# A decoder layer with 64 experts: the first gathers read the token names directly, and most first weights are loaded behind a wait for them

## The reference

```
x = x + self_attention(layernorm(x))
x = x + cross_attention(layernorm(x), ctx, mask)
x = x + ffn(layernorm(x))

ffn:  scores = softmax(x @ gate.T)                 # 64 experts, 8 groups, 3 groups and 6 experts kept
      buf[e, slot] = x[token]                      # at most 192 tokens of each expert
      out[e] = (silu(buf[e] @ Wg[e].T) * (buf[e] @ Wu[e].T)) @ Wd[e].T      # 512 -> 352 -> 512
      y = sum over the 6 experts of out[expert, slot] * weight
      shared = silu(x @ Sg.T) * (x @ Su.T) @ Sd.T  # 512 -> 704 -> 512, for every token
```

## Time and profile before

| what | value |
|---|---|
| median of the runs | 1560.71 us |
| profiled execution | 1567.02 us |
| its span | 1565.3 us |
| mean granted TensorE clock | 0.98 |
| TensorE busy | 1480.1 us (95%) |
| VectorE, ScalarE, GpSimd busy | 72%, 61%, 46% |
| DMA | 280.25 MB, mean 179 GB/s |

### The profile page before, as it was taken

How to read it: one execution, slowest core, us unless ns; L and a number is a source line. 1 busy time by engine, 2 the same in 40 slices (tenths; PEclk the granted TensorE clock), 3 DMA queues, 4 the chain that set the end, 5 groups by cost and what they waited for, 6 DMA issues and landing times.

```text
span 1565.3 us, 30313 instructions
## 1 busy us (share of the span) xinstructions
PE 1480.1 (95%) x10344; PEld 1223.1 (78%) x10344; DVE 1131.8 (72%) x2021; ACT 959.3 (61%) x1896; POOL 725.0 (46%) x896
## 2 busy tenths in 40 slices
PE   6999998999999988689999999999999999999988
PEld 4788886778888766479888888888888888876675
DVE  6677666646888788657777777777777777757756
ACT  4566565644566565568777877778777777741111
POOL 2122224333232154346556555565655655447663
PEclk9999999999999999789999999999999999999999
DMA  6012212322121221399877787777887778367664
GB/s 209 1 62 81 68 41 69 106 94 68 62 83 47 82 82 48 116 361 323 273 265 266 259 290 271 269 261 263 290 269 268 262 264 293 121 211 245 175 192 148
DMA packets 116629, 280.25 MB, mean 179 GB/s; under 512 B 17984, under 2 KB 23104, under 8 KB 116544
## 3 DMA queue, kind: packets, MB, share of 16 engines
q1 hardware_dynamic: 98800, 228.25, 42.9%
q0 software_dynamic: 15360, 50.34, 10.1%
q10 hardware_dynamic: 2384, 0.53, 0.2%
HBM read 235.69 MB, written 43.38 MB: 178 GB/s over the span
## 4 chain that ended last, share of the span: by engine, by line
PE 45%; DVE 4%; issue 2%; DMA 2%; SPq 1%; POOL 1%; another core or an unknown queue 1%; DVEq 1%; ACT 1%; POOLq 0%
PE e_gu L2606 18%; PE e_gu L2608 8%; PE e_dn_rest L2634 5%; PE e_dn_main L41 3%; PE e_tr L49 3%; PE e_dn_main L43 3%; PE e_dn_main L42 3%; DVE h_acc L2899 2%; DMA e_raw_u<-in_L_ffn_Wu_dram 1%; SPq L2314 1%; POOL h_yk L2816 1%; DVEq L2928 1%; PE h_dn L41 1%; PE h_dn L42 1%
## 5 line engine op out<-in xcount | busy, mean ns | idle before, releaser
L2369 POOL TENSOR_TENSOR e_hid<-e_h_raw,e_hid 128x128 fp32r<-128x128 f32 (+1 forms) x192 | 165.8, 864 | 224.0 <-ACT e_hid L2434 224.0
L2606 PE MATMUL e_gu<-e_xT_hi_lo,e_wg 128*128 128x384 f32 (+1 forms) x768 | 232.2, 358 | 2.4 <-DVE e_wu L2501 1.8
L2606 PE MATMUL e_gu<-e_xT_hi_lo,e_wu 128*128 128x384 f32 (+1 forms) x768 | 231.2, 356 | 0.0
L2608 PE MATMUL e_gu<-e_xT_hi_lo,e_wu 128*128 128x192 f32 (+1 forms) x768 | 193.5, 252 | 0.0
L2608 PE MATMUL e_gu<-e_xT_hi_lo,e_wg 128*128 128x192 f32 (+1 forms) x768 | 193.4, 252 | 0.0
L2377 POOL TENSOR_TENSOR e_wd<-e_raw_d,e_wd 96x512 fp32r<-96x512 f32 x64 | 131.5, 2055 | 36.1 <-ACT e_wd L2419 36.1
L2606 PEld LDWEIGHTS e_gu<-e_xT_hi_lo,e_wg 128*128 128x128 f32 (+1 forms) x768 | 138.3, 180 | 7.8 <-issue 3.7
L2429 ACT ACTIVATE e_low<-e_gu 128x384 f32<-128x384 f32 (+1 forms) x192 | 93.2, 485 | 81.7 <-PE e_gu L2608 73.8
L2512 DVE TENSOR_TENSOR e_total<-e_gu,e_low 128x384 f32<-128x384 f32 (+1 forms) x192 | 105.6, 550 | 51.9 <-issue 41.3
L2606 PEld LDWEIGHTS e_gu<-e_xT_hi_lo,e_wu 128*128 128x128 f32 (+1 forms) x768 | 138.4, 180 | 3.8
L2608 PEld LDWEIGHTS e_gu<-e_xT_hi_lo,e_wg 128*128 128x128 f32 (+1 forms) x768 | 140.2, 183 | 1.4
(11 more groups left out here) (425 smaller groups left out, 3964.4 us busy)
## 6 DMA issues: line engine op xcount, KB each, us to landing
e_raw_g<-in_L_ffn_Wg_dram SPq DMA_DIRECT2D x64, 704.0 KB, 4.3
e_raw_u<-in_L_ffn_Wu_dram SPq DMA_DIRECT2D x64, 704.0 KB
e_raw_d<-in_L_ffn_Wd_dram SPq DMA_DIRECT2D x64, 512.0 KB, 6.4
y_dram<-e_y_main SPq DMA_DIRECT2D x64, 256.0 KB, 7.9
e_raw_d<-in_L_ffn_Wd_dram SPq DMA_DIRECT2D x64, 192.0 KB, 7.6
y_dram<-e_y_rest SPq DMA_DIRECT2D x64, 128.0 KB
s_xr<-in_x_dram SPq DMA_DIRECT2D x16, 256.0 KB, 4.1
x_dram<-s_x SPq DMA_DIRECT2D x16, 256.0 KB, 2.8
```

The costliest lines, as they stand in the source:

```text
L2369: pool.tensor_tensor(hid[b][1][0:n, c, :], h_raw[g.odd][b][0:n, c, 0:P], hid[b][0][0:n, c, :].bitcast(F32), ALU.subtract).then_inc(s_hl, 1)
L2606: pe.matmul(bank[0:n, 0:2 * CAP], w[b][0][:, k, m:m + n], xT[:, :, k, toks], start=k == 0, stop=False)
L2608: ins = pe.matmul(bank[0:n, 0:CAP], w[b][1][:, k, m:m + n], xT[:, 0, k, toks], start=False, stop=k == KC - 1)
```

## The change

SyncE issues expert 0's gate and up weights, then waits until all three gathers of pair 0 have landed, and then issues gate and up of expert 1, the down weights of both experts, and gate and up of expert 2. For pair 0 the gathers take their addresses from `names` itself, without the copy to `idx` and the wait for it. The count that the later pairs wait for is lower by one accordingly. Nothing else differs.

```diff
@@ sync @@
+            load_gu(pair(0), 0, True)
+            for j in range(COLS):
+                sp.wait_ge(s_x[j], 16)
+            load_gu(pair(0), 1, True)
             for b in range(2):
-                load_gu(pair(0), b, True)
                 load_d(pair(0), b, True)
             load_gu(pair(1), 0, False)
@@ gather @@
                 n = g.n
+                ids = names
                 if not (isinstance(n, int) and n == 0):
-
+                    ids = idx
                     pool.wait_ge(s_t, COLS * (n - 1) + j1)
-                pool.tensor_copy(idx[:, j0:j1], names[:, bass.ds(n * COLS + j0, j1 - j0)]).then_inc(s_idx[part], 1)
-                pool.wait_ge(s_idx[part], n + 1)
+                    pool.tensor_copy(idx[:, j0:j1], names[:, bass.ds(n * COLS + j0, j1 - j0)]).then_inc(s_idx[part], 1)
+                    pool.wait_ge(s_idx[part], n)
...
-                                            in_offset=bass.IndirectOffsetOnAxis(ap=idx[:, j:j + 1], axis=0)
+                                            in_offset=bass.IndirectOffsetOnAxis(ap=ids[:, j:j + 1], axis=0)
```

## The result

The changed kernel takes 1564.83 us in the median (7 runs, 1563.07 to 1567.66), the kernel before 1559.66 us in the same rounds (7 runs, 1557.74 to 1561.35). The ratio is 1.0029, with a 95% interval of 1.0018 to 1.0039: slower by some 4.5 us (2.8 to 6.1); the two medians are 5.2 us apart. The forecast was 1562.6 us and +1.9 us, in a range of 1559.5 to 1566.0. The sign and the place were right, the size was under half of what was measured. A second timing of the same kernel later gave 1.0040 (1.0025 to 1.0055), with a median of 1567.56 us against 1560.77; that median would be above the upper end of the range.

The account below looks back on a forecast made before the run. The entrance was taken as bound by DMA bytes ahead of expert 3's weights: 1.97 us for missing bytes plus the resume delay gave +1.9 us, order and clock 0, so 1560.7 became 1562.6 us, range 1559.5 to 1566.0.

Parts of the forecast that it names:

- What bounds the entrance: Expert stage's entrance: full DMA queue, 366 GB/s from 665 to 700.79 us, ending in expert 3's weights; TensorE stops 1.83 us.
- TensorE's gain in front: Expert 0's gate/up matmuls: begin at 666.3 to 667.3 instead of 670.14 us, a gain of about 3.3 us.
- The index copies: Pair 0's gathers on GpSimd: without copies, first gather starts at 657.07 against 657.58, third at 659.7 against 660.54 us.
- The gathers' landing: Pair 0's third gather: lands 3.3 to 5.1 us after its start, 663.4 us taken, instead of 8.1 to 8.4 us.
- the prediction's own formula: Expert 3's weights land later by 1.97 + (L - 663.43) us, L being the third gather's landing; 1.9 us for L = 663.4.
- the rival in which the gathers stay slow: Pair 0's gathers: 8.4 us not caused by weights, L 668.1, shift 6.6 us, time 1567.3 us; chance 0.11.
- The moved order: SyncE's queue: expert 0's down weights behind expert 1's gate/up weights, same bytes ahead of expert 3; worth 0 on the path.
- The sum: Whole kernel: expert 3 starts at 704.08 + 1.9 = 706.0 us, nothing given back; median 1562.6 us, slower by 0.12%.
- The clock: TensorE after its stop before expert 3: about 7 us stop starts at 1.2 GHz level; counted 0, at most 0.3 us more.
- between, from 3.1 us up to 5.5: Expert 3's start: slower case between the forecast's own and the slow-gather rival, shift 3.1 to 5.5 us; chance 0.08.
- The case that the forecast was built on: Expert 3's start: weights land later by 1 to 3.1 us, 1.9 us taken; chance 0.56.
- What would show it: Entrance trace: third gather starts near 659.7, SyncE issues near 663.5, TensorE stops about 7 us, expert 3 near 706 us.

Follow-up runs that it names:

- wait_one: Against the changed kernel, SyncE waits for the first of the three gathers alone; ratio to the kernel before 1.0017 (1.0006 to 1.0029).
- wait_turned: Against the changed kernel, SyncE also waits until TensorE has transposed all three gathered tiles; ratio to the kernel before 1.0056 (1.0041 to 1.0072).
- the spread pair: Kernel before and changed kernel, each with the shared expert's 5.5 MB of loads spread over pairs 1 to 4; ratios to before 0.9977 and 0.9952.
- after_spread: Changed kernel with the shared expert's 5.5 MB issued in pieces after the turns of pairs 1 to 4; 1554.48 us against 1560.77, ratio 0.9952.
- e3: Not a run: time from SyncE's first expert load to TensorE's first matmul of expert 3; 48.79 us before, 51.42 us changed.
- before_again: The kernel before, unedited, timed and profiled a second time; ratio 0.9997 (0.9985 to 1.0010).
- names_only: Against the changed kernel, loads in the old order without SyncE's wait; only the first gathers' addresses come from names; ratio to before 1.0006, median 1561.06 us.
- order_only: Against the changed kernel, SyncE's wait removed, new order of loads kept; ratio to the kernel before 1.0025 (1.0012 to 1.0038), median 1563.83 us.
- pair 1: As a time, not a run: from SyncE's first expert load to the twelve rest matmuls of pair 1; 68.59 us before, 71.55 us changed.

## Why the prediction was right, and where it was short

*What bounds the entrance* was right: a queue full of bytes, ending in expert 3's weights, with a stop of TensorE behind it. wait_one against wait_turned and the spread pair show it from two sides, in the traces and in the times.

*TensorE's gain in front* was right: 3.3 us forecast; expert 1's matmuls began 21.47 us after the first load, against 24.90 (680.19 - 655.29), 3.4 us sooner. after_spread shows that it is real when nothing takes it back.

*The index copies* were wrong. I let the first gather start 0.5 us sooner because a copy and its wait were gone. It started 2.24 us after the first load in place of 2.29. In the old kernel it began 0.95 us after the last cast of the names had ended (656.63), with the copy in between; in the new one 0.90 us after it (659.16), with nothing in between. Something else holds the first gather for that time, and the copy lay beside it. Only the third gather gained its 0.2 us.

*The gathers' landing* was right in kind: 3.8 us for the third, in the bounds of the earlier trace rows, with 3.7 taken. By the start above it landed at 8.83 us after the first load, where I had 8.1. Put into the prediction's own formula (L = 655.29 + 8.83 = 664.12) this gives 1.97 + 0.69 = 2.7 us, and e3 was 2.63 us later than in the profile I predicted from. The agreement is in part luck: against before_again e3 was 4.0 us later and against names_only 4.5, and the formula knows nothing of the order, which has a cost of its own. The landing times also answer the rival in which the gathers stay slow as well: with no weights but expert 0's beside them, the 8 us become 4 to 5. "DMA: Bandwidth & Descriptors" of the Trainium skill, section "Queues, rings and completion order", has an engine take turns between its queues packet by packet; the landing times beside weights here are longer than my estimate of 4.0 us by that rule, and the 3.8 to 5.3 us with only expert 0's gate and up weights beside them show that the weights were the reason.

*The moved order* was put at 0 on the path, because it leaves the bytes ahead of expert 3 as they were. That was wrong. order_only was 3.3 us slower than names_only in the means, and its DMAs moved 0.40 MB less in 40 us: the same bytes, but not at the same rate. Expert 2's weights were not late, as forecast (in the changed kernel ScalarE was idle for 0.06 us before it took them up).

*The sum* fell short in size, by this term and by two more. The clock was priced at 0 to 0.3 us more. That nearly holds against the one profile I had, whose stop of 1.83 us had lowered the clock too (pair 1 came 19.80 us after e3, against 20.13 and 20.44 in the changed kernel). Against an execution such as before_again, with a stop of 0.78 us, the longer stop costs 1.8 to 2.1 us more than its length. The third is the base: that profile's e3 of 48.79 was a late one; before_again has 47.38 and names_only 46.89. 4.0 us of later start (51.42 - 47.38) and 1.8 us of clock are 5.8 us, against 2.6 and 0.3 from the other profile, and 6.2 us against names_only (71.55 - 65.31). The timed losses, 4.5 and 6.2 us (1.0029 and 1.0040), lie within these ends. That the runs of the kernel before divide between such executions is an inference from three profiles.

*The chances.* A shift of 4.5 us belongs to the case "between, from 3.1 us up to 5.5", which was given 0.08. The case that the forecast was built on, a shift of 1 to 3.1 us with 0.56, did not come.

*What would show it*: the signs named came, with the first off in place (third gather 5.04 us after the first load, not 4.4, and SyncE's issue at 8.92, not 8.2).

## What to carry to other kernels

Where a queue is full up to a late transfer, letting the engines pass it idle to help an early one only moves the stop: price a wait on the issuing engine by the bytes it keeps from moving, do not take a new order of the same bytes as free, and look first for bytes that need not be in the entrance at all. Read a short stall from more than one profile, since it, and the lowered clock behind it, may be there in one execution and not in the next. And moving bytes a few places back moves the stop with them; spread them over stretches with a spare rate.

## What the runs showed that I had not expected

- A stop of TensorE of 0.78 us left the granted clock at 1.00, stops of 1.83 and 2.32 us brought it to 0.56 in the 3.85 us after them, and with stops of 6 to 8 us it was 0.50 (the 1.2 GHz level). Beside their own length the stops of 1.83 and 2.32 us cost 1.4 to 1.5 us, and the long ones 1.8 to 2.8.
- The order of the same loads has a price: with both experts' down weights back to back the DMAs moved 298 GB/s in a stretch of 6 us, against 371 with the old order, and the timed runs were 3.3 us slower in the mean.
- The first indirect gather started 0.90 to 0.95 us after the names were ready, with an index copy in between or without one.
- The transfers are not lost one for one when the wait grows: from 8.8 to 11.75 us of waiting, expert 3 came 5.1 us later and not 3.0. The bytes missing after 44 us make 4.4 us of it; why the rate stayed lower after SyncE had gone on is not explained.
- Executions of the same program differed by 7 us after the experts' last matmul (188.5 and 181.4 us), more than the whole effect of the change.
